# A gated two-layer kernel in split fp32: batch 0's down-products formed as seven, the shared weight sums formed once, one gate in another PSUM bank

## The reference, cut to what matters

```python
# layer 0: a weight mixed per batch from 8, an elementwise mask, bias, residual
w_bot = einsum('bg,got->bot', cond, weight * mask);  x = x + einsum('bnt,bot->bno', x, w_bot) + bias
# layer 1: one shared MLP and the top 2 of 8 experts, for each of 4 batches of 512 tokens
mlp(x, g, u, d) = einsum('bsi,ih->bsh', gelu(x @ g) * (x @ u), d)      # 256 -> 1024 -> 256
x = x + mlp(x, shared) + sum_k w[b, k] * mlp(x, expert[sel[b, k]])
```

## Time and profile before

| | us |
|---|---|
| median of three runs (lowest, highest) | 416.71 (415.83, 416.97) |
| the profiled execution | 416.73 |
| its span, first to last instruction | 414.9 |
| PE busy | 409.4 (99%) |
| DVE, ACT, POOL busy | 262.1, 234.7, 256.7 (63%, 57%, 62%) |
| mean granted TensorE clock | 1.000 |

### The profile page before, as it was taken

One profiled execution on the slowest core, in us unless ns is written; L12 is line 12 of the kernel. 1 busy time (PEld: TensorE's weight loads), 2 busy tenths in 40 slices (PEclk: granted clock), 3 DMA queues, 4 the chain that ended last, 5 costly groups with the idle time before them and its releaser, 6 DMA issues.

```text
span 414.9 us, 7010 instructions
## 1 busy us (share of the span) xinstructions
PE 409.4 (99%) x2133; PEld 350.6 (85%) x2133; DVE 262.1 (63%) x452; ACT 234.7 (57%) x448; POOL 256.7 (62%) x275
## 2 busy tenths in 40 slices
PE   8999999999999999999999999999999999999997
PEld 5688888888888888888888888888888888888886
DVE  3556644244348877865767878775666675666684
ACT  5665454463425567665556566666465555766541
POOL 1565465378702459988533878998560885878630
DMA  7764324334200442243110053322300033222101
GB/s 241 244 199 108 96 81 126 98 102 104 76 25 9 122 126 76 77 134 96 42 38 0 25 177 90 112 76 76 101 25 25 0 117 87 78 92 87 40 12 51
DMA packets 20187, 36.24 MB, mean 87 GB/s; under 512 B 2242, under 2 KB 3010, under 8 KB 20162
## 3 DMA queue, kind: packets, MB, share of 16 engines
q1 hardware_dynamic: 19872, 35.66, 28.5%
q10 hardware_dynamic: 290, 0.26, 0.2%
HBM read 33.82 MB, written 2.10 MB: 87 GB/s over the span
## 4 chain that ended last, share of the span: by engine, by line
PE 96%; DMA 1%; DVE 1%; SPq 1%; issue 0%; ACT 0%; DVEq 0%
PE o_ps L563 12%; PE g_ps L505 11%; PE g_ps L504 11%; PE g_ps L508 10%; PE u_ps L505 10%; PE u_ps L508 10%; PE u_ps L504 10%; PE p_ps L563 9%; PE o_ps L556 8%; PE l_ps L463 2%; DMA l_raw<-l_w 1%; PE p_ps L444 1%; DVE t_raw L941 0%; PE o_ps L605 0%; SPq L276 0%
## 5 line engine op out<-in xcount | busy, mean ns | idle before, releaser
L1193 POOL TENSOR_TENSOR eg_lo<-raw_g,eg_hi 128x512 fp32r<-128x512 f32 x64 | 85.8, 1356 | 41.2 <-ACT eg_hi L711 41.2
L1000 DVE SCALAR_TENSOR_TENSOR u_ps<-gelu,route_cur,u_ps 128x512 f32<-128x512 f32 x64 | 48.3, 754 | 77.0 <-PE u_ps L508 77.0
L740 ACT ACTIVATE gelu<-g_ps 128x512 f32<-128x512 f32 x96 | 57.7, 601 | 59.7 <-PE g_ps L508 59.1
L505 PE MATMUL g_ps<-x_hi,eg_lo 128*128 128x512 f32 (+1 forms) x128 | 50.4, 394 | 0.0
L504 PE MATMUL g_ps<-x_hi,eg_hi 128*128 128x512 f32 (+1 forms) x128 | 50.1, 392 | 0.0
L505 PE MATMUL u_ps<-x_hi,eg_lo 128*128 128x512 f32 (+1 forms) x128 | 49.8, 389 | 0.0
L504 PE MATMUL u_ps<-x_hi,eg_hi 128*128 128x512 f32 (+1 forms) x128 | 49.8, 389 | 0.0
L762 ACT CAST h_hi<-u_ps 128x512 fp32r<-128x512 f32 x34 | 19.9, 587 | 49.8 <-DVE u_ps L1000 31.1
L1036 DVE TENSOR_TENSOR h_lo<-t_raw,h_hi 128x1024 fp32r<-128x1024 f32 x34 | 47.3, 1392 | 0.0
L995 DVE TENSOR_TENSOR u_ps<-gelu,u_ps 128x512 f32<-128x512 f32 x32 | 22.3, 696 | 31.2 <-PE u_ps L508 30.2
L1232 POOL TENSOR_TENSOR ed_lo<-raw_d,ed_hi 128x384 fp32r<-128x384 f32 x22 | 22.4, 1020 | 30.2 <-ACT ed_hi L720 30.2
(11 more groups left out here) (234 smaller groups left out, 1120.6 us busy)
## 6 DMA issues: line engine op xcount, KB each, us to landing
raw_g<-experts SPq DMA_DIRECT2D x64, 256.0 KB, 2.8
raw_d<-experts SPq DMA_DIRECT2D x32, 256.0 KB, 2.8
l_raw<-l_w SPq DMA_DIRECT2D x8, 256.0 KB, 5.7
x_in<-xT SPq DMA_DIRECT2D x8, 256.0 KB, 4.4
raw_g<-shared SPq DMA_DIRECT2D x8, 256.0 KB, 4.4
raw_d<-shared SPq DMA_DIRECT2D x8, 256.0 KB, 2.9
outT<-out_sb SPq DMA_DIRECT2D x6, 256.0 KB, 3.2
mask<-l_mask SPq DMA_DIRECT2D x2, 128.5 KB, 6.0
```

The costliest lines, as they stand in the source:

```text
L505: pe.matmul(ps, w_lo[:, at:at + P], x1_at(x1_hi, b, hh), start=False, stop=False)
L740: act.activation(gelu[:, s % 2], g_ps[:], ACT.Gelu_apprx_tanh).then_inc(gelu_done, 1)
L1000: dve.scalar_tensor_tensor(u_ps[:, s % 2], gelu[:, s % 2], route_cur[:, k:k + 1], u_ps[:, s % 2], ALU.mult, ALU.mult).then_inc(h_done, 1)
L1193: pool.tensor_tensor(eg_lo[:, j % RING], raw_g[:, j % RAW_G], eg_hi[:, j % RING].bitcast(F32), ALU.subtract).then_inc(gu_lo_done, 1)
```

## The change

Every pair of batch 0 becomes a fast pair. The shared sums are formed from the first load of the shared down weights and kept, so the second load and its steps go; POOL and ACT get a new order for batch 0 (`chunks_at`), SP one to match; the plain path, `store_ready_0` and their semaphores go, and batch 0 ends like batches 1 and 2. The gate of chunk 1 goes to `l0_ps` and no longer waits for the first gelu. In the counts of semaphores the seeds and the "b - 1" disappear; these lines are left out below.

```diff
         def fast(b, p):
-            return not at_first(b) and not (at_last(b) and p >= LAST_FAST)
+            return not (at_last(b) and p >= LAST_FAST)
...
+        def chunks_at(s):
+            if s == 1:
+                return range(4, 5)
+            if s == 3:
+                return range(5, 7)
+            if s == 5:
+                return range(7, 10)
+            return range(s + 3, min(s + 5, CHUNKS + ECH))
...
+            def shared_weights():
+                for c in range(FIRST):
+                    shared_gu(c)
+                shared_d(0)
+                shared_gu(3)
+                shared_gu(4)
+                shared_d(1)
+                shared_gu(5)
+                shared_gu(6)
+                shared_d(2)
+                shared_gu(7)
+                sp.wait_ge(x_hi_done, HH)
+                sp.wait_ge(x_lo_done, HH)
+                for hh in range(HH):
+                    load_x_half(1, hh)
+
             def batch_0():
+                sp.wait_ge(indexed, B)
                 e = expert_of(0, 0)
-                for j in range(5):
-                    load_gu(0, j, e)
+                load_gu(0, 0, e)
+                load_gu(0, 1, e)
+                shared_d(3)
+                load_gu(0, 2, e)
+                load_gu(0, 3, e)
                 load_d(0, 0, e)
+                load_gu(0, 4, e)
                 load_gu(0, 5, e)
                 load_d(0, 1, e)
...
-                shared_d_again(0)
...
-                for hh in range(HH):
-                    sp.wait_ge(out_done, hh + 1)
-                    sp.dma_start(outT[0, :, hh], out_sb[:, hh]).then_inc(stored, 16)
+                store(0)
...
+            def gate_ps(b, s):
+                return l0_ps if at_first(b) and s == 1 else g_ps
...
-                pe.wait_ge(gelu_done, n)
-                project(g_ps, w_hi, w_lo, GATE, b).then_inc(g_done, 1)
+                if at_first(b) and s == LAG:
+                    pe.wait_ge(gelu_done, 1)
+                elif not at_first(b) or s > LAG:
+                    pe.wait_ge(gelu_done, n)
+                project(gate_ps(b, s), w_hi, w_lo, GATE, b).then_inc(g_done, 1)
...
             def products_123(b, p):
                 wait_d(b, p)
                 pe.wait_ge(h_lo_done, STEPS * b + 2 * p + 2)
-                if p == 0:
+                if first_pair(b, p):
                     pe.wait_ge(x1_done, HH)
-                    pe.wait_ge(out_done, 1)
-                    pe.wait_ge(evac_done, 4 * b)
+                elif p == 0:
+                    pe.wait_ge(evac_done, 4 * b - 2)
...
@@ scalar engine (ACT) @@
             def split_shared_d(i):
                 act.wait_ge(raw_d_in[i % RAW_D], 16 * (i // RAW_D + 1))
-                act.copy(sd_hi[:, i, 0:W2], raw_d[:, i % RAW_D]).then_inc(d_hi_done, 1)
+                act.copy(sd_hi[:, i, 0:3 * P], raw_d[:, i % RAW_D, 0:3 * P]).then_inc(d_hi_done, 1)
             def split_shared_s(i):
-                act.wait_ge(down_done, 2 * i + 2)
                 act.wait_ge(s_raw_done, 4 * i + 4)
...
             def split_b11(b, p):
                 n = STEPS * b + 2 * p
                 act.wait_ge(h_done, n + 1)
-                act.wait_ge(down_done, n - 1)
+                if not first_pair(b, p):
+                    act.wait_ge(down_done, n - 1)
+                    act.wait_ge(t_done, 4 * pair_count(b, p))
                 act.copy(h_hi[:, 0:TH], u_ps[:, 0, 0:TH]).then_inc(h_hi_done, 1)
-                if not (isinstance(b, int) and b == 1 and p == 0):
-                    act.wait_ge(t_done, 4 * pair_count(b, p))
                 act.copy(b12[:], u_ps[:, 0, TH:T]).then_inc(b12_done, 1)
...
             def weights_beside(b, s):
                 if at_first(b):
...
+                    if s == 0:
+                        split_shared(FIRST)
+                    if s % 2:
+                        for c in chunks_at(s):
+                            if c < CHUNKS:
+                                split_shared(c)
+                            else:
+                                split_gu(0, c - CHUNKS)
+                    if s % 2 == 0 and 0 < s < CHUNKS:
+                        split_shared_d(s // 2)
+                        split_shared_s(s // 2)
...
             split_shared_d(0)
-            for s in range(2):
-                step(0, s, False)
-                first_x1(s)
+            activate(0, 0)
+            split_b11(0, 0)
+            weights_beside(0, 0)
+            activate(0, 1)
+            split_shared_s(0)
+            split_b2(0, 0)
+            first_x1(0)
+            weights_beside(0, 1)
+            first_x1(1)
             batch(0, True)
...
@@ gpsimd engine (POOL) @@
             def shared_s(i):
-                d = s_index(i)
-                pool.wait_ge(raw_d_in[d % RAW_D], 16 * (d // RAW_D + 1))
+                pool.wait_ge(raw_d_in[i % RAW_D], 16 * (i // RAW_D + 1))
                 if i > 0:
-                    pool.wait_ge(d_lo_done, s_index(i - 1) + 1)
-                form_s(i, raw_d[:, d % RAW_D])
+                    pool.wait_ge(d_lo_done, i)
+                form_s(i, raw_d[:, i % RAW_D])
+            def split_shared_d(i):
+                pool.wait_ge(d_hi_done, i + 1)
+                pool.tensor_tensor(sd_lo[:, i, 0:3 * P], raw_d[:, i % RAW_D, 0:3 * P], sd_hi[:, i, 0:3 * P].bitcast(F32), ALU.subtract)
                 pool.wait_ge(s_hi_done, i + 1)
                 pool.tensor_tensor(sd_lo[:, i, S1 * P:7 * P], s_raw[:], sd_hi[:, i, S1 * P:7 * P].bitcast(F32), ALU.subtract).then_inc(d_lo_done, 1)
...
             def batch_0():
...
+                for c in range(FIRST):
+                    split_gate(c)
+                    split_up(c)
+                shared_s(0)
+                split_shared(FIRST)
+                split_shared_d(0)
+                for s in range(1, STEPS):
+                    if s % 2:
+                        p = (s + 1) // 2
+                        if p < PAIRS:
+                            shared_s(p)
+                        elif p < NP:
+                            expert_s(0, p - PAIRS)
+                        for c in chunks_at(s):
+                            if c < CHUNKS:
+                                split_shared(c)
+                            else:
+                                split_gu(0, c - CHUNKS)
+                    elif s < CHUNKS:
+                        split_shared_d(s // 2)
+                    else:
                         split_d(0, (s - CHUNKS) // 2)
                     next_beside(0, s)
+                sum_products(0)
```

More of the change, by code:

```diff
@@ L381, in batch @@
                         load_gu(b + 1, j, n)
-                    for hh, sums in ((0, SUMS - 1), (1, SUMS)):
-                        sp.wait_ge(sum_done, SUMS * (b - 1) + sums + 1)
-                        sp.dma_start(outT[bass.ds(b, 1), :, hh].rearrange("a p t -> (a p) t"), out_sb[:, hh]).then_inc(stored, 16)
+                    store(b)
                 else:
@@ L401, in _ @@
                 sp.dma_start(mask[:, oh], l0_mask[oh]).then_inc(mask_in[oh], 16)
[L402 to L413, removed]
+            shared_weights()
             batch_0()
@@ L530, in gate_up, with rest_down @@
                     pe.wait_ge(gu_lo_done, s + 1)
[L531 to L538, removed]
+                if not (at_first(b) and s < 2):
+                    if s % 2 and (s < 2 or fast(b, s // 2 - 1)):
+                        pe.wait_ge(t_done, 4 * pair_count(b, s // 2 - 1) + 4)
+                    else:
+                        pe.wait_ge(h_lo_done, n - 1)
                 project(u_ps[:, s % 2], w_hi, w_lo, UP, b).then_inc(u_done, 1)
             def wait_d(b, p):
[L542 to L545, removed]
-            def plain_down(b, s, psums, first, last):
-                n = STEPS * b + s
-                wh, wl = d_weights(s // 2)
-                hh_, hl_ = h_slot(b, s)
-                wait_d(b, s // 2)
-                pe.wait_ge(h_lo_done, n + 1)
+                pe.wait_ge(d_lo_done, p + 1 if p < PAIRS else d_index(b, p - PAIRS) + 1)
+            def rest_down(s):
+                wh, wl = d_weights(s // 2)
+                hh_, hl_ = h_last(s)
+                wait_d(B - 1, s // 2)
+                pe.wait_ge(h_lo_done, STEPS * (B - 1) + s + 1)
+                pe.wait_ge(x1_done, HH * B)
+                pe.wait_ge(rest_done, 1)
                 for oh, blk in enumerate((A12, A22) if s % 2 else (A11, A21)):
                     for i, (w, x) in enumerate(((wh, hh_), (wh, hl_), (wl, hh_))):
-                        mm = pe.matmul(psums[oh], block_of(w, blk), x, start=(first and i == 0), stop=(last and i == 2))
-                    if last and oh == 0:
-                        mm.then_inc(sum0_done, 1)
+                        mm = pe.matmul(LAST_PS[oh], block_of(w, blk), x, start=(i == 0), stop=(i == 2))
                 mm.then_inc(down_done, 1)
@@ L580, in products_4567 @@
                 pe.wait_ge(t_lo_done, pair_count(b, p) + 1)
-                if p == 0:
```

(19 more changed lines are left out.)

151 lines of the change are left out of this document (41 added, 110 removed).

## The result

The changed kernel takes 418.49 us (median of five, 416.81 to 418.54) against 416.62 for the kernel before: ratio 1.0039, 95% interval 1.002 to 1.0058. It is slower, by 1.9 us; I had forecast 415.2 and a range from 414.1 to 416.7.

What follows compares the result with a forecast made beforehand. PE, busy 99% of the span, was taken as the bound. PE's work -2.05, start +0.05, chunk 5 +0.25, DVE +0.25 and later batch 0 0 sum to -1.5 us: 415.2 from 416.73, range 414.1 to 416.7.

Steps and rivals of the forecast that it cites:

- PE's work: Batch 0's plain pairs of 8.16 us become fast pairs of 8.00, and a wait at batch 1 goes: -2.05 us.
- The start: Before down(0,0): chunk 1's freed gate gains at most 0.61 us, lost to the wait for x1; start at 25.1, net +0.05.
- Chunk 5: Its gate in batch 0 waits for POOL's late remainder: PE loses some 0.25 us, bounds 0 and 1.0.
- DVE at step 4: In batch 0, routing operations held by POOL's running operations delay DVE before down(0,4): 0.25 us more, bounds 0 and 1.0.
- POOL is short: Rival, chance 0.26: through the front of batch 0, chunk 5, routing and down 5 and 6 come late; 416.4 us.
- The thin margin at down 6: Batch 0, steps 9 to 12: POOL's remainder ready at 73.5, needed at 73.6; taken as 0, upper bound +1.0 us.
- Slower: Rival, chance 0.06: POOL becomes the bound, every pair of batch 0 costing it 8.9 us; 418.9 us.

Runs made afterwards that it cites:

- all_fixed_phase: Changed kernel with routing moved early, x1 copied out earlier, POOL's batch 0 order mended, and 57 instructions of met waits on PE; 414.18 us, ratio 0.9928.
- after_phase: Changed kernel with 57 more instructions (already met waits) on PE's queue in batch 0; 416.82 us, ratio 0.9999.
- x_in_place_phase: all_fixed_phase with the splits of x for batch 1 back at steps 9 and 11, ahead of the next steps' down remainders; 414.42 us, ratio 0.9951.
- after_again: The changed kernel run once more with nothing altered; 418.27 us, ratio 1.0041.

## Why the prediction was wrong

**PE's work: right.** A fast batch takes 98.72 us, so the saving of 2.05 is real, and `all_fixed_phase` shows it for batch 0. The products in `all_fixed_phase` stand 0.12 apart. The isolated gap of the Trainium skill ("TensorE: Matmul & The Clock Gate", section Back-to-back issue gap), 109 ns for 256 columns, by which the batch would have saved 3.6, does not hold for them.

**The start: right.** down(0,0) at 25.01 against the forecast 25.1, released by `first_x1(1)`; the gate's bank gives 0.6 there and x1 takes it. (The wait that the prediction puts before the up product of chunk 1 is before its gate: the row says `g_ps`.)

**Chunk 5: right in place, 0.43 in place of 0.25.** The idle 0.17 in brackets is near my number; I did not count that a matmul after a wait is slower.

**The first failed step is "DVE at step 4": its term of 0.25 measured 1.8.** It priced the lock for L916 and L918 at step 4 and two operations at step 5 (2.2 and 0.4; they took 2.2 and 0.4) and stopped there. It left out that `route_weigh` has two more operations at step 6, behind the next `split_t`, which meets POOL's list at its densest (three chunks in step 5). What I took for 0.25 at down(0,4) was 0 there, and 1.8 at down(0,5), up(8) and down(0,6). (Its own figures, 2.3 against a slack of 1.9 with PE 0.25 late, give 0.15.) Its upper bound of 1.0 was too low for the same reason. The rule from the earlier trace rows was right; I applied it to two of three places. The trace of the kernel before had the third place too: L926, the first of the two, lasts 0.46 there for 8 elements and ends with a POOL operation, 42.70 beside 42.67, while L928 right behind it meets no POOL operation and takes 0.17.

```profile
42.24 0.46 DVE L926 TENSOR_SCALAR pair_rest<-pair 128x8 f32<-128x8 f32 x1
42.73 0.17 DVE L928 SCALAR_TENSOR_TENSOR route_w<-pair,pair_rest 128x8 f32<-128x8 f32 x1
```

```profile
41.38 1.29 POOL L1193 TENSOR_TENSOR eg_lo<-raw_g,eg_hi 128x512 fp32r<-128x512 f32 x1 [1.55 <-ACT eg_hi L711]
```

With 1.8 the sum is -2.05 - 0.03 + 0.43 + 1.8 = +0.15, and the trace's span moved by +0.1.

**The second failed step is the end of the kernel, which the sum leaves as it was.** The prediction adds its sum to the 416.73 of before and takes what comes after the last matmul for unchanged, without a reason. Nothing in it looks at the length of PE's program, though the change adds nine matmuls to every pair of batch 0. It is the larger part of the result: of 1.9 us slower, 1.7 come from there, and without them (`after_phase`) the change is within 0.1% of before.

**The rivals.** *POOL is short* came nearest in time (416.4 against 416.8 with the short tail) with the wrong engine: POOL gave 0.43, and down 5 and 6 were in time. So its nearness is luck. The thin margin at down 6 is borne out in `x_in_place_phase`, where PE gets there 2.9 us earlier. *Slower* happened, but not by the mechanism that I priced. That 40 us more on POOL and 34 on DVE leave batches 1 to 3 alone was right.

## What to carry to other kernels

Before an engine gets more work beside another, list every operation of either that holds the SBUF port both share, the tiny ones first: the price of one was here the rest of the neighbour's running instruction, not its own length; move such operations to where the neighbour is idle, or let one input come from PSUM. When a list of dependent work is costed by hand, walk it to its end with the rule found, and do not stop at the first place that it explains. And when executions of one kernel fall in two groups, compare the tails of the two traces, instruction transfers included, before taking the medians for the worth of the change: padding one engine's program to another length is a cheap control.

## What the runs showed of the hardware that I had not expected

An instruction transfer of 16 KB beside the last 128 KB store costs that store 1.6 us (3.6 in place of 2.0 from issue to landing, in three traces). 192 instructions without any work, far from the end, make the kernel before slower by as much, 418.30 against 416.74 us; the tail itself was not traced there. The Trainium skill ("Runtime: NRT & Kernel Launch", section Instruction fetch mechanics) says that a sequencer fetches its program in blocks of 16 KiB, 256 instructions, through a DMA queue of its own, at a cost that is mostly hidden. The size agrees: 0.02 MB in each packet of q8, and one packet more for the longer programs. "Mostly hidden" agrees too: the other 13 transfers of `after_again` come before 389 us, and from 52 us to its last matmul PE has no gap. Where the last transfer is not hidden, it is 0.4% of the kernel.
